# The adapter of a four-stage transformer kernel: own columns and stacked rows in place of a product with all adapters

## The reference

```python
x = x + L0(x)          # per sample one of 200 matrices, over the token axis
x = x + L1(x)          # attention, window of 256 keys out of a paged pool, new keys and values written into it
x = x + L2(x)          # per sample one of 16 experts: x @ W[id] + b[id]
x = x + L3(x)

def L3(x):             # adapter_idx: one of 8 adapters for each sample, rank 16
    H = einsum('btd,od->bto', x, W)
    xa = einsum('btd,brd->btr', x, A[adapter_idx])
    delta = einsum('btr,bor->bto', xa, Bm[adapter_idx]) * scalings[adapter_idx]
    return H + delta
```

## Time and profile before

| | |
|---|---|
| median of 3 runs | 1035.92 us (1035.61 to 1037.2) |
| the profiled execution | 1039.95 us |
| its span | 1038.1 us |
| granted TensorE clock | 0.985 of full |
| busy, share of the span | PE 96%, PEld 69%, DVE 64%, ACT 52%, POOL 52% |
| DMA | 196.17 MB, mean 189 GB/s |

### The profile page before, as it was taken

One profiled execution on the slowest core, in us unless ns is written; L12 is line 12 of the kernel. 1 busy time (PEld: TensorE's weight loads), 2 busy tenths in 40 slices (PEclk: granted clock), 3 DMA queues, 4 the chain that ended last, 5 costly groups with the idle time before them and its releaser, 6 DMA issues.

```text
span 1038.1 us, 24050 instructions
## 1 busy us (share of the span) xinstructions
PE 999.5 (96%) x6438; PEld 714.4 (69%) x6438; DVE 660.5 (64%) x1928; ACT 537.7 (52%) x1337; POOL 542.8 (52%) x597
## 2 busy tenths in 40 slices
PE   8998999999768999999999999999999999999998
PEld 6676777767635777766777766677766677777666
DVE  5897898666744656556656556655655665565562
ACT  4347776667444544455445455554545545544551
POOL 3553644446675555556555555656645555555500
PEclk9999999999969999999999999999999999999999
DMA  4333453365447767777677777767777776777650
GB/s 142 115 126 125 137 171 126 104 201 190 148 123 224 211 194 240 229 205 245 205 215 228 219 202 224 219 196 232 223 213 197 233 210 205 216 237 205 201 201 21
DMA packets 95338, 196.17 MB, mean 189 GB/s; under 512 B 31346, under 2 KB 40114, under 8 KB 87110
## 3 DMA queue, kind: packets, MB, share of 16 engines
q1 hardware_dynamic: 63942, 149.49, 45.8%
q0 software_dynamic: 30784, 44.16, 15.5%
q10 hardware_dynamic: 576, 2.10, 0.6%
HBM read 195.08 MB, written 33.56 MB: 220 GB/s over the span
## 4 chain that ended last, share of the span: by engine, by line
PE 68%; issue 1%; POOL 1%; DMA 1%; DVE 0%; ACT 0%; POOLq 0%; SPq 0%; DVEq 0%; ACTq 0%
PE bank L93 15%; PE bank L1506 12%; PE bank L1460 9%; PE bank L1481 9%; PE bank L1468 8%; PE bank L1556 6%; PE bank L1436 4%; PE bank L1447 3%; PE bank L1560 3%; DMA W<-in_w 1%; POOL KV L1152 0%; DMA KVE<-in_pool,idxs_e 0%; POOL KVE L1162 0%; POOL KV L1162 0%; PE bank L1527 0%
## 5 line engine op out<-in xcount | busy, mean ns | idle before, releaser
L1266 ACT ACTIVATE PR<-SM,nb 128x336 f32<-128x336 f32 x256 | 147.5, 585 | 6.5 <-DVE nb L1338 6.3
L1162 POOL DMA_INDIRECT KV<-kv_scratch,idxs x96 | 96.6, 1007 | 101.0 <-DMA KV<-in_pool,idxs 77.0
L1162 POOL DMA_INDIRECT KVE<-kv_scratch,idxs_e x93 | 93.4, 1004 | 95.6 <-DMA KVE<-in_pool,idxs_e 71.0
L1257 ACT ACTIVATE PT<-bank 112x384 f32<-112x384 f32 x256 | 111.4, 489 | 56.1 <-PE bank L1468 55.1
L1506 PE MATMUL bank<-W,XT 128*64 128x512 f32 x512 | 126.2, 609 | 3.7 <-DMA W<-in_w 3.7
L1152 POOL DMA_INDIRECT KV<-in_pool,idxs x96 | 98.8, 1029 | 49.2 <-issue 24.8
L1152 POOL DMA_INDIRECT KVE<-in_pool,idxs_e x90 | 92.9, 1032 | 54.5 <-issue 30.0
L93 PE MATMUL bank<-wqh,XTH 128*128 128x512 f32 x256 | 106.5, 416 | 9.0 <-DVE XTL L506 6.0
L1468 PE MATMUL bank<-ident,PR 128*112 128x128 f32 x768 | 108.8, 278 | 2.6 <-DVE PR L1345 2.6
L1468 PEld LDWEIGHTS bank<-ident,PR 128*112 128x112 f32 x768 | 83.5, 134 | 34.4 <-DVE PR L1345 19.8
L93 PE MATMUL bank<-wql,XTH 128*128 128x512 f32 x256 | 101.8, 398 | 0.0
(11 more groups left out here) (204 smaller groups left out, 2338.0 us busy)
## 6 DMA issues: line engine op xcount, KB each, us to landing
W<-in_w SPq DMA_DIRECT2D x64, 1024.0 KB, 5.6
X<-in_x SPq DMA_DIRECT2D x32, 256.0 KB, 2.9
x_scratch<-X SPq DMA_DIRECT2D x32, 256.0 KB, 2.0
qt_scratch<-QT SPq DMA_DIRECT2D x32, 256.0 KB, 2.9
XB<-x_scratch SPq DMA_DIRECT2D x32, 256.0 KB
BB<-in_b SPq DMA_DIRECT2D x64, 128.0 KB
out_dram<-XO SPq DMA_DIRECT2D x32, 256.0 KB
kv_scratch<-KVR SPq DMA_DIRECT2D x31, 256.0 KB, 3.1
```

The costliest lines, as they stand in the source:

```text
L1162: pool.indirect_dma_start(out=KV[k][:, c, :], out_offset=None, in_=kv_d, in_offset=bass.IndirectOffsetOnAxis(ap=idxs[k][:, NCH + c:NCH + c ...
L1257: return nc.scalar.activation(dst, src, ACT.Copy)
L1266: nc.scalar.activation(PR[u % 2][:, :], SM[u % 2][:, :], ACT.Exp, bias=nb[:, u:u + 1], scale=SCALE, accum_out=rs[:, u:u + 1]).then_inc(s_e, 1)
```

## The change

The product with the columns of all adapters and the mask behind it are given up.

- `AS` in SBUF holds each adapter's 16 columns four times over (64 columns for each of the 4 blocks of features). `bs_d` in DRAM holds each adapter's 16 rows of B (scaled already) four times: twice the high part, twice the low part. Both are made at the end of stage 1.
- For each pair SP issues four transfers, behind the `store` and ahead of `weights(1)`: two of 128 KB from `AS` to `AG` (SBUF to SBUF) and two of 128 KB from `bs_d` to `BG`.
- `adapter` becomes 8 fp32 products (4 blocks, 2 samples) of 64 columns with 64 columns stationary; `adapted_sum` becomes one fp32r product of 128 by 512, and stands after the first half of `output`.
- ScalarE makes a second, exact copy `XT3` of the turned x behind the high part; VectorE's low part is taken from `XT3`.
- VectorE makes `XAH`, `XAM` and two small combinations `XA` in place of mask and split.
- The late weights have four parts of 1024 columns to split in place of five, and an extra copy for A and B.

```diff
@@ stage 1
+                def scale_b():
+                    dve.wait_ge(s_wlate, 16 * 6)
+                    v.tensor_scalar(b_raw, b_raw, scal[:, 0:1], None, ALU.mult).then_inc(s_bsc, 1)
+
+                def adapter_low():
+                    dve.wait_ge(s_wlh, 3)
+                    split(BSH, BSL, b_raw).then_inc(s_wl, 1)
-                between.update({27: late_low(0), 28: late_low(1), 29: late_low(2),
-                                31: in_turn(late_low(3), late_low(4))})
+                between.update({27: late_low(0), 28: late_low(1), 29: adapter_low, 30: late_low(2), 31: late_low(3)})
+                def store_b():
+                    sp.wait_ge(s_wl, 3)
+                    for g in range(4):
+                        sp.dma_start(bs_d[:, g], (BSH, BSL)[g // 2].bitcast(F32)).then_inc(s_bso, 16)
+                def adapter_high():
+                    act.wait_ge(s_bsc, 1)
+                    copy(AS[:, :, :, :], a_raw.rearrange("p (e r) -> p e r", r=RANK).unsqueeze(2).to_broadcast(
+                        [P, NA * KC, 4, RANK]))
+                    copy(BSH, b_raw).then_inc(s_wlh, 1)
@@ SyncE, stage 2
+                    def adapter_columns(q):
+                        numbers = [sp.value_load(aid[0:1, bass.ds(q * 2 + b, 1)], min_val=0, max_val=NA - 1)
+                                   for b in range(2)]
+                        wait(sp, s_xa, q)
+                        for b, e in enumerate(numbers):
+                            sp.dma_start(AG[:, b, :], AS[:, :, :, :].rearrange("p (e k) s r -> p e (k s r)", e=NA)
+                                         [:, bass.ds(e, 1)].rearrange("p o c -> p (o c)")).then_inc(s_ag, 16)
+                        wait(sp, s_l3, q)
+                        for b, e in enumerate(numbers):
+                            sp.dma_start(BG[b * T:(b + 1) * T, :].bitcast(F32), bs_d[bass.ds(e, 1)]
+                                         .rearrange("o g r n -> (o g r) n")).then_inc(s_bg, 16)
                     if adapted:
                         store(pr.move(-2))
+                    if dense:
+                        adapter_columns(p - 1)
@@ ScalarE
                         copy(XTH3[:, :, :].rearrange("p k t -> p (k t)"), bank[7][:, :]).then_inc(s_xt3h, 1)
+                        copy(XT3[:, :, :].rearrange("p k t -> p (k t)"), bank[7][:, :]).then_inc(s_xt3f, 1)
@@ VectorE
+                        dve.wait_ge(s_xt3f, at(r, 1, 0))
                         dve.wait_ge(s_xt3h, at(r, 1, 0))
-                        low(XTL3[:, :, :].rearrange("p k t -> p (k t)"), bank[7][:, :],
-                            XTH3[:, :, :].rearrange("p k t -> p (k t)")).then_inc(s_xt3, 1)
+                        low(XTL3[:, :, :], XT3[:, :, :], XTH3[:, :, :]).then_inc(s_xt3, 1)
+                        v.tensor_copy(XAH[:, :], xa).then_inc(s_xah, 1)
+                        v.tensor_scalar(XAM[:, :], xa, sel[:, 1:2], None, ALU.mult).then_inc(s_xam, 1)
+                        for b in range(2):
+                            rows = slice(b * T, (b + 1) * T)
+                            v.scalar_tensor_tensor(XA[rows, rows], XAH[rows, :].bitcast(F32), sel[rows, 0:1],
+                                                   XAM[rows, :], ALU.mult, ALU.add).then_inc(s_xal, 1)
@@ TensorE
                 def adapter(r, of):
-                    pe.wait_ge(s_xt3, at(r, 1, 0))
-                    exact_products(mm, bank[of][:, 0:P], [(a_h[:, k, :], a_l[:, k, :], *x3t[k]) for k in range(KC)],
-                                   True, True).then_inc(s_xa, 1)
+                    pe.wait_ge(s_xt3f, at(r, 1, 0))
+                    pe.wait_ge(s_ag, at(r, 32, 31))
+                    for k in range(KC):
+                        for b in range(2):
+                            rows = slice(b * T, (b + 1) * T)
+                            last = mm(bank[of][rows, 0:T], AG[:, b, k * T:(k + 1) * T], XT3[:, k, rows],
+                                      start=k == 0, stop=k == KC - 1, skip_group_check=True)
+                    last.then_inc(s_xa, 1)
 
                 def adapted_sum(r, of):
-                    pe.wait_ge(s_xal, at(r, 1, 0))
-                    exact_products(mm, bank[of][:, :], [(XAH[:, :], XAL[:, :], b_h[:, 0, :], b_l[:, 0, :])],
-                                   False, True).then_inc(s_l3, 1)
+                    pe.wait_ge(s_xal, at(r, 2, 1))
+                    pe.wait_ge(s_bg, at(r, 32, 31))
+                    mm(bank[of][:, :], XA[:, :], BG[:, :], start=False, stop=True).then_inc(s_l3, 1)
@@ TensorE, body
-                        dense3_low()
-                        adapted_sum(r, 6)
+                        dense3_low(r)
                     if dense:
-                        if adapted:
-                            pe.wait_ge(s_xam, at(r, 1, 0))
-                        output(q, 0, KC)
+                        if adapted:
+                            pe.wait_ge(s_xah, at(r, 1, 0))
+                            pe.wait_ge(s_xam, at(r, 1, 0))
+                        output(q, 0, 2)
+                    if adapted:
+                        adapted_sum(r, 6)
+                    if dense:
+                        output(q, 2, KC)
```

More of the change, by code:

```diff
@@ L137, in build @@
         FM_e = [early[:, D + i * SPAN:D + (i + 1) * SPAN] for i in range(2)]
-        NWL = KC * D * 2 + KC * P + D
+        NWL = KC * D * 2
+        NWR = NWL + KC * P + D
         wlh = sb("wlh", [P, NWL], F32R)
         wll = sb("wll", [P, NWL], F32R)
+        AS = sb("AS", [P, NA * KC, 4, RANK])
         def late(tile, which):
-            a, n = {"wo": (0, D), "w3": (KC * D, D), "a": (2 * KC * D, P), "b": (2 * KC * D + KC * P, D)}[which]
-            k = 1 if which == "b" else KC
-            return tile[:, a:a + k * n].rearrange("p (k n) -> p k n", k=k)
+            a = {"wo": 0, "w3": KC * D}[which]
+            return tile[:, a:a + KC * D].rearrange("p (k n) -> p k n", k=KC)
         s_const = sem("const_ready")
@@ L287, in build @@
             phys = flat[:, 0:SPAN].rearrange("p (m u) -> p m u", u=BLOCK)
+            BSH, BSL = (trig[:, :, :, :].rearrange("p a b c -> p (a b c)")[:, i * D:(i + 1) * D].bitcast(F32R)
+                        for i in range(2))
             none, some = (trig[0:CH, 3 + i, :, :].rearrange("p b c -> p (b c)")[:, 0:NCH * NB] for i in range(2))
@@ L484, in indices @@
                     yield
-                    step(v.tensor_scalar(pns[:, :], pni[:, :], 4, None, ALU.arith_shift_right))
+                    step(v.tensor_scalar(pns[:, :], pni[:, :], 4, 1, ALU.arith_shift_right, ALU.bitwise_and))
                     yield
@@ L489, in indices @@
                     yield
-                    step(v.tensor_copy(adf[:, :], adi[:, :]))
+                    step(v.tensor_copy(sel[:, 1:2], pnf[:, 0:1]))
                     yield
-                    step(v.tensor_scalar(adapt[:, :], adf[:, :], pnf[:, 0:1], scal[:, 0:1], ALU.is_equal, ALU.mult))
+                    step(v.tensor_scalar(sel[:, 0:1], sel[:, 1:2], -2.0, 1.0, ALU.mult, ALU.add))
                     yield
@@ L922, in _ @@
                 bodies(act, body, {6: lambda: sines(2, EARLY, PAIRS)} |
[L923 removed]
+                       {26: in_turn(late_high(0), late_high(1)), 27: adapter_high, 28: late_high(2), 29: late_high(3)})
             @block.tensor
@@ L1379, in body @@
                         dve.wait_ge(s_xa, at(r, 1, 0))
[L1380 to L1383, removed]
+                        xa = bank[1 if last_dense(p) else 7][:, 0:T]
+                        v.tensor_copy(XAH[:, :], xa).then_inc(s_xah, 1)
+                        v.tensor_scalar(XAM[:, :], xa, sel[:, 1:2], None, ALU.mult).then_inc(s_xam, 1)
+                        dve.wait_ge(s_xah, at(r, 1, 0))
                         dve.wait_ge(s_xam, at(r, 1, 0))
-                        v.tensor_copy(XAH[:, :], xam).then_inc(s_xah, 1)
-                        dve.wait_ge(s_xah, at(r, 1, 0))
-                        low(XAL[:, :], xam, XAH[:, :]).then_inc(s_xal, 1)
+                        wait(dve, s_l3, r)
+                        for b in range(2):
+                            rows = slice(b * T, (b + 1) * T)
+                            v.scalar_tensor_tensor(XA[rows, rows], XAH[rows, :].bitcast(F32), sel[rows, 0:1],
+                                                   XAM[rows, :], ALU.mult, ALU.add).then_inc(s_xal, 1)
                     if attention:
@@ L1431, in _ @@
                 wo_h, wo_l, w3_h, w3_l = late(wlh, "wo"), late(wll, "wo"), late(wlh, "w3"), late(wll, "w3")
-                a_h, a_l, b_h, b_l = late(wlh, "a"), late(wll, "a"), late(wlh, "b"), late(wll, "b")
                 def turn_x(tile, s_done):
```

47 lines of the change are left out of this document (31 added, 16 removed).

## The result

The changed kernel takes **1091.68 us** (median, 1088.09 to 1093.01) where the kernel before takes 1036.56 in the same comparison: 1.052 times as long, 95% interval 1.0481 to 1.0557. The prediction was 1055 us with 1010 to 1080 around it, so the direction came, but the time lies above the range and the loss is nearly three times the predicted one: +55 us, not +19. The profiled execution took 1090.65 us, its span 1088.6.

A forecast was written before the change was run, and what follows sets the result against it. POOL's gather chain was taken to bound stage 2, its beat growing from 22.0 to 23.3 us: 28 bodies against 22.53 give +21.6, less 2.65 in the tail, +18.9 us, so 1055 us, range 1010 to 1080.

The forecast's parts named there:

- Which chain bounds: Stage 2: POOL's gather chain needs 22.0 us a body beside TensorE's 22.53; after the change TensorE runs at POOL's beat.
- The growth of the landing: First sample's gathers in stage 2: 512 KB more behind the matrix delay their landing by 1.3 us (0 to 3.3).
- Where it showed: POOL's chain in stage 2: first landings of 6.5 to 7.5 us, second averaging 8.3, 4.0 for each sample's remaining gathers.
- rival 3: Queues take fair turns, so a gather is held up at most 0.65 us: beat 22.65, 1036.6 us, chance 0.09.
- Number of bodies: Stage 2: 28 bodies (3 to 31) at 23.3 us in place of 22.53, +21.6 us.
- End of stage 1 and tail: End of stage 1: one split less, -0.6 us (-1.2 to 0); tail without gathers: TensorE's gain, -2.65 us.
- rival 1: TensorE stays the bound and keeps all its gain of 35.8 us: 1000 us, chance 0.08.
- narrow products: The adapter's 8 new fp32 products, 16 instructions on TensorE: 0.74 us in place of 1.38, saving 0.64 (0.21 to 0.94).
- Arrival of `AG`: AG lands 8.0 us after the first matrix is issued (7.1 to 8.6), so TensorE waits at the adapter in every body.
- TensorE's body: Stage 2: 22.53 us less 0.64 for narrow products and 0.46 for the stacked product gives 21.43.
- ScalarE, VectorE, SP at nothing: Stage 2: ScalarE's extra 0.60 us copy is covered, VectorE's smaller operations and SP's extra issues cost nothing.
- The signs named in the prediction: Profile signs: PE waits 1 to 2 us a body for AG, POOL never for PE, first matrices 23.3 us apart.

The follow-up runs named there:

- i1: Changed kernel with the four transfers made for the first pair only, that pair's columns and rows used for all: 1026.51 us, 0.991 of before.
- i2: Kernel before plus one transfer of 512 KB a pair with rows of 4 KB, nothing computing with it: 1060.57 us, 1.0233 of before.
- i3: Changed kernel with two buffers each of AG and BG, the next pair's four transfers issued behind the second expert matrix: 1043.46 us, 1.0078 of before.
- h4: Changed kernel with two buffers each of AG and BG, fetched one pair earlier at the same place in SP's queue: 1091.19 us, 1.0532 of before.
- h1: Kernel before plus the four transfers a pair at the changed kernel's place, nothing computing with them: 1091.12 us, 1.0532 of before.
- f1: Changed kernel, unaltered, rerun on a chip where the kernel before took 1159.92 us: 1115.24 us.

## Why the prediction was right in direction and wrong in size

- **Which chain bounds: right.** The prediction had POOL with its landings at 22.0 us a body and TensorE slaved to it. i1 shows 22.04 without transfers, and between the two stores of the changed kernel POOL waits for TensorE once, 1.83 us.
- **The growth of the landing: the step that failed.** 512 KB at 3.1 us a MB, three quarters of it: 1.3 us a pair. From the floor of 22.04 to 24.27 it was 2.2: against i1, 1.9 in the first landing (6.08 to 7.97), 0.5 in the rests (8.18 to 8.69), -0.2 in the second landing. The term is wrong in two ways. The load's duration was taken by bytes alone. For one transfer with rows of 4 KB the sum came out (i2: 23.26 - 22.0 = 1.3, the predicted beat of 23.3), for the transfers as they are it did not: 2.6 us of DMA time in place of 1.5. Whether their rows or their number is the reason stays open. And the slope was drawn through two landings that differ in more than the KB behind the matrix: by it i3, with 1104 + 512 KB behind the second matrix, would have a second landing of 8.3 + 1.6 = 9.9. It has 7.26. KB in the queue don't set a landing by a line; the place of the same transfers counts (i3 against h4), and that it counts through the time of issue relative to the gathers is the reading of i3's rows.
- **Where it showed.** First landing 7.97, predicted 7.0; second 7.57, predicted 8.3; the rest of both samples 8.69, predicted 8.0, because POOL now waits for its later gathers too, 0.7 us a body (0.1 before, 0.3 in i1). Of rival 3: the page "DMA: Bandwidth & Descriptors" (Queues, rings and completion order) of the Trainium skill has queues take turns by packet, from which a cap of 0.65 us was worked out. The first landing grew by 7.97 - 5.36 = 2.6 against the kernel before, and by 1.9 against i1. The same page says that a turn is a packet of several descriptors, and no row here shows the size of one; so the rule isn't refuted, but the cap worked out from it, one gather's own size for each queue, is.
- **Number of bodies.** 28 bodies were charged, from the third on. The second store is already 4.5 us late, though POOL's first `held` gather of stage 2 starts 1.1 us early (294.08 against 295.20): the transfers begin with body 1. That is some two bodies more. 30 x 1.83 = 54.9, less 1.1 and 3.4 for the two ends, is 50.4 of the +50.5.
- **End of stage 1 and tail: the numbers came, what they were meant for isn't shown.** -1.1 lies in the bounds of -1.2 to 0. But h1 and i2, with the stage 1 of the kernel before, start that gather at 292.94 and 293.05, earlier still, and i1, with the changed one, at 296.01: the spread between executions covers the term. The tail is -3.4 for -2.65. But h1, whose TensorE has the whole old adapter to do, has 50.5 us behind that store, less than the changed kernel's 51.0, so this isn't TensorE's gain alone.
- **Sums.** Two small slips, neither of weight: two and a half adapters at 1.10 are 2.75 and not 2.65, and rival 1 with narrow products at their upper bound would be 1014 and not 1010.
- **Arrival of `AG`: late by more than thought**, with no effect on the time (h4). It was issued at 529.60 and let TensorE go at 537.85, 10.65 us after the matrix, predicted 8.0.

```profile
537.85 1.12 PE L1571 MATMUL bank<-XT,AG 128*64 128x64 f32 x16 [3.80 <-DMA AG<-AS]
538.76 1.49 PE L1532 MATMUL bank<-PT,KV 112*64 112x128 f32 x12
540.19 1.49 PE L1511 MATMUL bank<-KT,early 64*128 64x336 f32 x4
```

- **TensorE's body: right.** Predicted 21.43, seen 21.3 in one body without a wait (i1). The narrow products were predicted at 0.74 and are cheaper, the stacked product is where it was put:

```profile
561.77 0.40 PE L1613 MATMUL bank<-wll,XTH 128*128 128x512 f32 x1
562.10 0.69 PE L1571 MATMUL bank<-XT,AG 128*64 128x64 f32 x16
562.61 0.83 PE L1532 MATMUL bank<-PT,KVE 112*64 112x128 f32 x12
...
567.48 0.40 PE L1578 MATMUL bank<-BG,XA 128*128 128x512 f32 x1
567.72 0.39 PE L93 MATMUL bank<-wlh,OTH 128*128 128x512 f32 x1
```

  562.61 - 562.10 = 0.51 us for 16 instructions, plus 0.10 by which the product ahead lasts longer than its 0.23: 0.61. The page "TensorE: Matmul & The Clock Gate" (section LDWEIGHTS) of the Trainium skill, from which 0.85 was estimated for loads in sequence, has 53 ns for a load of 64 columns; these rows, where the loads take turns between two halves of the array, have 32 ns for load and product together, and the measurement decides.
- **ScalarE, VectorE, SP at nothing: right.** TensorE's waits for probabilities stay where they were, and h1 has the whole loss without any of these steps.
- **The signs named in the prediction**: waits of PE for a DMA into `AG`, 1 to 2 us a body, came with 63.0 us in all, 2 a body; POOL waits for TensorE once; first landings were to be 6.5 to 7.5 and are 8.0; the transfers were to land within 9 us of the matrix, and one took 10.65.

## What to carry to other kernels

Where two chains run at nearly the same beat, price a change on the one that it doesn't seem to touch: here 1.1 us a body were taken from TensorE, and adding the transfers alone to the kernel before costs 54 us of the 55. A transfer that nobody waits for is not free if it is issued while another engine's gathers are under way; ask of each new DMA what is in flight when it is issued. And don't price it by KB alone: the same 512 KB a pair cost 2.3 us a body as four transfers, 1.2 as one with long rows, and 0.6 as four at another place. Before adding a copy, look for a wait of 2 to 4 us that is there anyway: the kernel with the copies behind such a wait took 63 us longer than with the same copies ahead of it.

## What the runs showed of the hardware

- The same 512 KB took 2.6 us of all 16 DMA engines' time as four transfers with rows of 1 and 2 KB, and 1.5 us as one with rows of 4 KB.
- A matmul of 64 columns stationary and 64 moving in fp32, alternating between two halves of the array, took 32 ns an instruction (0.51 us for 16, load included) at the full granted clock.
- After a wait of 3.80 us TensorE's next products took 1.12 and 1.49 us instead of 0.69 and 0.83, at a granted clock of 0.50 (1.2 GHz) from 537.85 to 541.68 us; the mean of that execution was 0.958. The waits for `AG`, 25 of up to 4.7 us, cost no time of their own here: without them, at a mean clock of 0.973, the kernel takes the same time (h4).
- On three of the chips the kernel before took 1127 to 1160 us in the median, and the changed one, on one of them, 1115. There the loss of 5% was not to be seen: the changed kernel took 1105 to 1116 in three executions, the kernel before 1122 in its fastest of seven. f1's trace shows waits with no releaser in the core.
